# The threshold search over three engines, and a last attention step without its detour

## The chip, the cores and the metric

The kernel runs on one core of one Trainium2 chip. The time is that of one execution on the device, in microseconds (us). Three runs of the kernel before gave 870.73, 871.9 and 873.82 us, so the median is 871.9 us. TensorE is called PE below (its weight loads PEld), VectorE DVE, ScalarE ACT, GpSimd POOL, and SP issues the transfers.

## The reference, cut to what matters

Four layers, each an attention and a feed-forward part, are added to `x` (2 batches of 256 rows of 512 numbers). The change touches the third attention, and the search of the fourth attention that runs beside it.

```python
# third attention: 32 query heads of 128, 8 groups of keys and values, 512 context rows
q = rmsnorm((layernorm(x) @ q_proj_w.T).reshape(B, Q, 32, 128).transpose(0, 2, 1, 3))
k = rmsnorm(k of 8 groups, each repeated 4 times);  v = likewise, not normed
attn = softmax(q @ k.T * scale + mask)
x = x + concat_heads(attn @ v) @ o_proj_w.T
...
# fourth attention: for each of 512 columns, the 154 largest of the 512 context rows;
# those among the first 256 rows are the "crucial" channels
_, topk_idx = jax.lax.top_k(jnp.moveaxis(channel_map, 1, 2), 154)
```

The products of the third attention are done in three passes over a high and a low part of each operand (`PARTS`), both of type float32r.

## The kernel before, in words

**Steps.** `layer2_attention` (L1542) works in 16 steps, one for each of 8 head groups and 2 batches. Even and odd steps are the two batches of one group; the first (step 0) and the last (step 15) are written out, and steps 1 to 14 are a loop of seven bodies, each an odd and an even step (on DVE six bodies, then steps 13 and 14 written out). A step has 8 units: 4 heads by 2 tiles of 128 queries. For a unit, PE computes scores (`scores`, L1808), DVE adds the mask and takes the maximum (`maximum`, L2070, instruction L2075), ACT takes the exponentials and their sums (`exponentials`, L1960, L1966), PE turns the 128x512 probabilities with four transposes (`turn_probs`, L1821, L1826), ACT copies the turned ones out of PSUM as the high part (`probsT_high`, L1974) and DVE subtracts for the low part (`probsT_low`, L2087). After two units (one head, a pair) PE multiplies them with the values (`mix`, L1830), in the one bank `V`.

**Beside a step.** In the same units PE projects keys and values (`project_kv`), then queries (`project_q`) of the following step, and the heads of the step before onto `x` (`project_out`, L1784); `fill` (L1839) fixes the unit of each. PE turns the normed rows of keys and queries of the following step (`turn_rows`, L1799) through the one bank `R`. ACT copies and squares the projections (`copy_kv`, `copy_q`), POOL norms them (`norm`, L1678), ACT and DVE split the turned ones (`rowsT_high` L1956/L1958, `rowsT_low` L2065/L2068). ACT also takes high parts of the following weights (`kv_weights_high`, `q_weights_high` L1990, `o_weights_high`), and POOL subtracts for their low parts (L1665, L1669, L1675).

**Division.** The probabilities are divided after the mix. At unit 7 DVE inverts the eight sums (`invert`, L2081), SP stores the inverses in DRAM and loads them back spread over all partitions, ACT copies the mixed heads to SBUF (`copy_mixed`, L1980), and POOL multiplies and splits them into high and low (`scale_heads`, L1696, L1700, L1702), two heads at a time. `project_out` then runs in the following step. After step 15 this chain stands alone at the end, with 24 products of PE behind it and two additions to `x` (`add_out`, L2093).

**The search.** For each of 8 row tiles of the transposed context (128x512), DVE finds the value of the 154th largest by bisection on bits. A round is four `bisection_count`s (L2240) of two tiles, one instruction per tile (L2244: compare and sum), and a `bisection_update` (L2289) of five small instructions, of which L2294, L2296, L2298 and L2301 have two inputs in SBUF. There is one count per unit and an update in every fourth unit: two rounds a step, 28 in steps 0 to 13, one in step 14, and those ahead of the steps. Then `choose_piece` (L2260) marks the chosen ones, 5 pieces for each pair of tiles (L2267, L2271, L2275, L2278, L2282): the first pair in units 4 to 7 of step 14, the other three pairs in step 15.

**Order.** Each engine has its own queue in a fixed, handwritten order; a waiting instruction holds all behind it. On ACT, unit u runs: row copies and splits of the following step, `copy_mixed`, the exponentials of unit u+1, `probsT_high` of unit u, weight copies. On DVE: `probsT_low` of u-1, `rowsT_low`, the maximum of u+1, values, `add_out`, and the search last. On PE: the fill, `turn_probs` of u, scores of u+2 (from unit 6 on those of the following step, which need `rowsT_low` of the rows), `mix`, `turn_rows`. `LoopOwn` numbers the steps of the search on one semaphore.

## Time and profile before

| | us |
|---|---|
| median of 3 runs | 871.9 |
| span of the profiled execution | 875.2 |
| steps 1 to 14, one pair of steps | 65.8 to 67.3 |
| last step, from the last transposes of step 14 (741.7) to the last addition (792.9) | 51.2 |
| tail behind it, to the end | 82.3 |

The page of the profile gives PE 783.4 us busy (90% of the span), DVE 719.1 (82%), ACT 519.3 (59%) and POOL 428.5 (49%). In its 40 slices of 21.9 us, PE stands at 9 tenths or more from slice 13 to slice 34, then falls to 5 and 7 tenths, which is the last step:

```profile
PE   1976899858987999999999999999999999578878
DVE  7878998968788888888888888887887887955974
ACT  6864898747466756756656756756656656321421
POOL 3237087805226647646646746646646746531110
```

A busy digit tells only that an engine had work in a slice; which wait ends last must be read from the timeline of the instructions on either side of it.

### The profile page before, as it was taken

The numbers are of one execution on the slowest core, as the hardware profiler recorded it, in microseconds if no ns is written. First come the engines' busy times: TensorE is split into PE (matmuls) and PEld (weight loads), VectorE is DVE, ScalarE is ACT, GpSimd is POOL, SyncE is SP. The second block draws the span as 40 slices with busy tenths as digits, with TensorE's granted clock in tenths as the row PEclk, the third lists the DMA queues.
The fourth block names the chain that finished last, engine by engine and source line by source line (L and its number), as shares of the span: only waits on it lengthen the run. The fifth ranks groups of instructions, "written<-read, shape, count | busy, mean of one in ns | idle before, by whom it ended". The sixth has DMA issues, their size and how long they took to land. (4 is left out here: it accounts for less than half of the span.)

```text
span 875.2 us, 16429 instructions
## 1 busy us (share of the span) xinstructions
PE 783.4 (90%) x5146; PEld 634.7 (73%) x5146; DVE 719.1 (82%) x1732; ACT 519.3 (59%) x1408; POOL 428.5 (49%) x380
## 2 busy tenths in 40 slices
PE   1976899858987999999999999999999999578878
PEld 0474676534776898898898897898898898465446
DVE  7878998968788888888888888887887887955974
ACT  6864898747466756756656756756656656321421
POOL 3237087805226647646646746646646746531110
PEclk9999999979999999999999999999999999789899
DMA  8253246562203102102102202201200300103001
GB/s 304 93 193 121 75 150 207 163 187 80 96 2 97 50 26 95 50 24 96 48 24 80 64 24 74 70 24 52 92 24 28 116 24 25 48 25 117 1 0 49
DMA packets 39114, 68.23 MB, mean 78 GB/s; under 512 B 5729, under 2 KB 18593, under 8 KB 38946
## 3 DMA queue, kind: packets, MB, share of 16 engines
q1 hardware_dynamic: 39074, 67.73, 23.5%
q8 instruction: 21, 0.34, 0.2%
q14 instruction: 19, 0.16, 0.1%
HBM read 62.38 MB, written 5.34 MB: 77 GB/s over the span
## 5 line engine op out<-in xcount | busy, mean ns | idle before, releaser
L1966 ACT ACTIVATE layer_attention_probs<-xnT,stats 128x512 f32<-128x512 f32 x128 | 93.9, 734 | 137.8 <-DVE stats L2075 137.8
L2244 DVE TENSOR_SCALAR_CACHE_REDUCE xn<-ctxT,candidate 128x512 bf16<-128x512 f32 x240 | 168.8, 741 | 0.0
L1750 PE MATMUL bank<-layer_attention_keysT,layer_attention_queriesT 128*128 128x512 f32 x384 | 122.6, 428 | 5.0 <-DVE layer_attention_queriesT L2068 5.0
L2087 DVE TENSOR_TENSOR layer_attention_probsT<-bank,layer_attention_probsT 128x512 fp32r<-128x512 f32 x128 | 88.0, 688 | 39.8 <-ACT layer_attention_probsT L1974 38.3
L1750 PEld LDWEIGHTS bank<-layer_attention_probsT,layer_attention_values 128*128 128x128 f32 x768 | 99.7, 191 | 23.0 <-DVE layer_attention_probsT L2087 9.3
L1750 PE MATMUL bank<-layer_attention_probsT,layer_attention_values 128*128 128x256 f32 x768 | 103.4, 284 | 14.0 <-DVE layer_attention_probsT L2087 13.9
L1750 PE MATMUL bank<-layer_attention_wo,layer_attention_headsT 128*128 128x512 f32 x384 | 104.5, 417 | 3.0 <-issue 3.0
L1974 ACT CAST layer_attention_probsT<-bank 128x512 fp32r<-128x512 f32 x128 | 74.7, 584 | 50.4 <-PE bank L1826 50.1
L1696 POOL TENSOR_TENSOR layer_attention_mixed<-layer_attention_mixed,xnT 128x512 f32<-128x512 f32 x32 | 52.1, 1627 | 86.3 <-DMA xnT<-inverse_sums 82.8
L1750 PE MATMUL bank<-layer_attention_l_wq,layer_attention_xnT 128*128 128x512 f32 x384 | 93.5, 392 | 0.0
L1750 PE MATMUL bank<-layer_attention_l_wkv,layer_context_parts 128*128 128x256 f32 x720 | 90.5, 278 | 0.0
L1750 PEld LDWEIGHTS bank<-layer_attention_l_wkv,layer_context_parts 128*128 128x128 f32 x720 | 88.5, 188 | 2.7
L2075 DVE CUSTOM_DVE_ANT_0 xnT<-bank,layer_attention_mask 128x512 f32<-128x512 f32 x128 | 87.0, 680 | 0.6 <-PE bank L1750 0.5
L1750 PEld LDWEIGHTS bank<-layer_attention_wo,layer_attention_headsT 128*128 128x128 f32 x384 | 71.6, 196 | 17.5 <-issue 3.1
L1750 PEld LDWEIGHTS bank<-layer_attention_l_wq,layer_attention_xnT 128*128 128x128 f32 x384 | 70.9, 188 | 15.0 <-issue 0.2
L1826 PE MATMUL bank<-ident,layer_attention_probs 128*128 128x128 f32 x512 | 78.1, 276 | 3.6 <-ACT layer_attention_probs L1966 3.6
L1826 PEld LDWEIGHTS bank<-ident,layer_attention_probs 128*128 128x128 f32 x512 | 62.5, 142 | 15.2 <-issue 4.8
L1750 PEld LDWEIGHTS bank<-layer_attention_keysT,layer_attention_queriesT 128*128 128x128 f32 x384 | 63.7, 193 | 11.6 <-issue 5.8
L1681 POOL TENSOR_SCALAR layer_attention_ssq<-layer_attention_ssq 128x4 f32<-128x4 f32 x48 | 9.3, 193 | 90.6 <-ACT layer_attention_squares L1925 90.6
L1925 ACT ACTIVATE layer_attention_squares<-bank 128x128 f32<-128x128 f32 x192 | 51.9, 298 | 0.0
L1170 ACT ACTIVATE layer_attention_probs<-bank,layer_attention_negmax 128x512 f32<-128x512 f32 x64 | 44.9, 706 | 10.6 <-DVE layer_attention_negmax L1066 10.3
L1669 POOL TENSOR_TENSOR layer_attention_l_wq<-layer_attention_l_raw_qo,layer_attention_l_wq 128x2048 fp32r<-128x2048 f32 x8 | 36.9, 4616 | 28.3 <-ACT layer_attention_l_wq L1990 28.3
(322 smaller groups left out, 1673.0 us busy)
## 6 DMA issues: line engine op xcount, KB each, us to landing
layer_attention_l_raw_qo<-in_wqT SPq DMA_DIRECT2D x9, 1024.0 KB, 5.1
xnT<-inverse_sums SPq DMA_DIRECT2D x16, 512.0 KB, 3.7
layer_attention_l_raw_qo<-in_woT SPq DMA_DIRECT2D x8, 1024.0 KB, 7.1
tw_raw<-in_w_gateT SPq DMA_DIRECT2D x8, 688.0 KB, 5.2
tw_raw<-in_w_upT SPq DMA_DIRECT2D x8, 688.0 KB, 4.2
tw_raw<-in_w_downT SPq DMA_DIRECT2D x6, 768.0 KB, 4.7
layer_attention_l_raw_kv<-in_wkvT SPq DMA_DIRECT2D x9, 512.0 KB, 4.8
ternary<-tw_rounded SPq DMA_DIRECT2D x8, 344.0 KB, 2.6
```

Source lines behind the costliest of these rows:

```text
L1170: a.activation(probs[:, u % 4, :], S[u % 3][:, :], ACT.Exp, bias=negmax[:, tile(u), head(u):head(u) + 1], accum_out=sums[:, tile(u), head( ...
L1669: g.tensor_tensor(wq[:, 1], gw.raw_q[:, :, :], wq[:, 0], ALU.subtract).then_inc(gw.q_low, 1)
L1681: own(g.tensor_scalar(ssq[:, c, :], ssq[:, c, :], 1.0 / HD, EPS, ALU.mult, ALU.add))
L1696: g.tensor_tensor(now, now, factors, ALU.mult).then_inc(S_["mix_scaled"], 1)
L1750: last = pe.matmul(out, stationary[f][a], moving[f][b], start=f == 0 and x == 0, stop=f == count - 1 and x == 2)
L1826: last = pe.transpose(T[u % 2][:, c * P:(c + 1) * P], probs[:, u % 3, c * P:(c + 1) * P], k.ident[:, :])
L1925: return a.activation(squares[:, h, :], source, ACT.Square, accum_out=ssq[:, c, h:h + 1])
L1966: a.activation(probs[:, u % 3, :], masked[:, u % 2, :], ACT.Exp, bias=negmax[:, u:u + 1], scale=-1.0, accum_out=sums[:, u:u + 1]).then_inc ...
L1974: a.copy(probsT[:, 0, p % 2, :, u % 2 * P:(u % 2 + 1) * P], T[u % 2][:, :].rearrange("p (c q) -> p c q", c=CPB)).then_inc(S_["probsT_high" ...
L2075: v.tensor_tensor_reduce(masked[:, u % 2, :], S[u % 2][:, :], mask[:, u % TPB, :], -1.0, 3.4e38, ALU.add, ALU.min, negmax[:, u:u + 1]).the ...
L2087: v.tensor_tensor(probsT[:, 1, p % 2, :, columns], T[u % 2][:, :].rearrange("p (c q) -> p c q", c=CPB), probsT[:, 0, p % 2, :, columns], A ...
L2244: own(k.nc.vector.tensor_scalar((k.flags if flags is None else flags)[:, r % 2], row_tile(k.ctxT, r), k.candidate[:, r:r + 1].bitcast(F32) ...
```

## The change

- **Search in steps 1 to 10** (`SEARCHED` = 5 loop bodies of two steps). A body of 16 units has 5 rounds of 3 units, and unit 15 has none. DVE counts six tiles (`BY_DVE` = 3 counts). POOL compares the last two (`compare_aside`: two instructions, flags in bfloat16, in a new tile `aside`), and ACT sums the flags (`count_aside`: two activations with a sum). POOL's compare of round 0 is its first work of the odd step, that of round 1 stands behind `norm(following, 0)`, that of round 2 behind `norm(following, 1)`, that of round 3 behind `scale_heads` of the even step, that of round 4 behind its `norm(following, 0)`. ACT's sums stand behind `probsT_high` of units 0, 4 and 7 (odd step) and 2 and 5 (even step). DVE waits for them ahead of each update.
- **Steps 11 and 12**: one round each, a count in every second unit, the update in unit 7. **Steps 13 and 14**: the choice, two pairs of tiles a step, pieces at `u * 10 // 8`. Step 15 has neither. The number of rounds is the same (2 + 25 + 2 = 29).
- **Last step** (`run_final`). For each unit DVE inverts one column of sums and multiplies the identity by it (`divided`: a reciprocal, a wait for it, a 128x128 `diagonal`); PE turns the probabilities with a plain float32 product by that diagonal (`turn_divided`) in place of the transpose. The mix then comes out divided: ACT copies it from bank `V` as the high part (`head_high`), DVE subtracts (`head_low`), and PE projects head by head (`project_final`: 2 tiles by 3 products). SP's round trip, `copy_mixed` and `scale_heads` go for this step. `project_out` of step 14 stands in units 5 and 6.
- **Last output weights.** They come as a ninth group of the query weights (`wqT`), in place of a repeat of the first that was loaded and not used; the loads and splits of the last `woT` group go (SP, ACT L1996, POOL L1675).
- The loops of ACT and POOL are split in two, of 5 and 2 bodies; on DVE steps 11 to 14 are written out. `dynamic_dma_scratch_size` is set to 1024.

```diff
+    SEARCHED = 5
+    ROUNDS = 5
+    SLOTS = 3
+    BY_DVE = 3
-    CHOICE = {STEPS - 2: (0,), STEPS - 1: (2, 4, 6)}
+    CHOICE = {STEPS - 3: (0, 2), STEPS - 2: (4, 6)}
...
@@ gpsimd
+                def compare_aside(step, r):
+                    g.wait_ge(S_["bisection"], step[0] * OWN_BODY + (OWN_LOOP + r * ROUND_OPS))
+                    g.sem_inc(S_["stepped"], 1)
+                    for j in range(2):
+                        row = 2 * BY_DVE + j
+                        last = g.tensor_scalar(aside[:, j], row_tile(k.ctxT, row), k.candidate[:, row:row + 1].bitcast(F32), 1.0,
+                                               ALU.is_gt, ALU.mult)
+                    last.then_inc(S_["aside_flags"], 1)
...
+                    if searching and odd:
+                        compare_aside(step, 0)
                     if not first:
                         scale_heads(before, 0)
                         scale_heads(before, 1)
+                    if searching and not odd:
+                        compare_aside(step, 3)
                     if odd:
                         o_weights_low(step, 0)
-                    if not last:
-                        norm(following, own, KEYS)
+                    norm(following, own, KEYS)
                     if odd:
                         o_weights_low(step, 1)
-                    if last:
-                        return
                     norm(following, own, 0)
+                    if searching:
+                        compare_aside(step, 1 if odd else 4)
                     if not odd:
                         kv_weights_low(step)
                     norm(following, own, 1)
+                    if searching and odd:
+                        compare_aside(step, 2)
...
@@ tensor
+                def turn_divided(step, u):
+                    pe.wait_ge(S_["probsT_low"], at(step, UNITS, u - 1))
+                    pe.wait_ge(S_["diagonal_ready"], u + 1)
+                    for c in range(CPB):
+                        last = pe.matmul(T[u % 2][:, c * P:(c + 1) * P], probs[:, u % 3, c * P:(c + 1) * P],
+                                         diagonal[:, u % 2, :], start=True, stop=True)
+                    last.then_inc(S_["probsT_psum"], 1)
+
+                def project_final(step, h):
+                    pe.wait_ge(S_["final_low"], h + 1)
+                    for t in range(TPB):
+                        if h == 0:
+                            pe.wait_ge(S_["out_added"], added(after(step, -1), t + 1))
+                        for x, (a, b) in enumerate(PARTS):
+                            last = pe.matmul(J[t][:, :], finalT[:, a, h, t * P:(t + 1) * P], wq[:, b, h, :],
+                                             start=h == 0 and x == 0, stop=h == REP - 1 and x == 2)
...
+                def run_final(step):
+                    before = after(step, -1)
+                    for u in range(UNITS):
+                        turn_divided(step, u)
+                        if u + 2 < UNITS:
+                            scores(step, u + 2)
+                        if u == 0:
+                            mix(before, PAIRS - 1)
+                        if u in (3, 5, 7):
+                            mix(step, u // 2 - 1, final=True)
+                        if u in (5, 6):
+                            for half in range(2):
+                                project_out(before, u - 5, half, weights=wq)
+                    project_final(step, 0)
+                    mix(step, PAIRS - 1, final=True)
+                    for h in range(1, REP):
+                        project_final(step, h)
...
@@ scalar
+                def count_aside(step, r):
+                    a.wait_ge(S_["aside_flags"], step[0] * ROUNDS + (r + 1))
+                    for j in range(2):
+                        row = 2 * BY_DVE + j
+                        last = a.activation(aside[:, j], aside[:, j], ACT.Copy, accum_out=k.counts[:, row:row + 1])
+                    last.then_inc(S_["aside_counted"], 1)
...
+                def run_final(step):
+                    before = after(step, -1)
+                    for u in range(UNITS):
+                        if u == 1:
+                            copy_mixed(before, PAIRS - 1)
+                        if u + 1 < UNITS:
+                            exponentials(step, u + 1)
+                        probsT_high(step, u)
+                        if u in (3, 5, 7):
+                            head_high(step, u // 2 - 1)
+                    head_high(step, PAIRS - 1)
...
                         probsT_high(step, u)
+                        if searching and odd and u in (0, 4, 7):
+                            count_aside(step, (0, 4, 7).index(u))
+                        if searching and not odd and u in (2, 5):
+                            count_aside(step, 3 + (2, 5).index(u))
...
@@ vector
+                    r, part = divmod((step[1] - 1) * UNITS + u, SLOTS)
+                    if r < ROUNDS:
+                        bisection_count(k, own, part)
+                        if part == SLOTS - 1:
+                            v.wait_ge(S_["aside_counted"], step[0] * ROUNDS + (r + 1))
+                            bisection_update(k, own)
...
+                def divided(step, u):
+                    v.wait_ge(S_["exp_ready"], at(step, UNITS, u + 1))
+                    v.reciprocal(last_inverse[:, u:u + 1], sums[:, u:u + 1]).then_inc(S_["last_inverted"], 1)
+                    v.wait_ge(S_["last_inverted"], u + 1)
+                    v.tensor_scalar(diagonal[:, u % 2, :], k.ident[:, :], last_inverse[:, u:u + 1], None, ALU.mult)\
+                     .then_inc(S_["diagonal_ready"], 1)
...
+                def run_final(step):
+                    before = after(step, -1)
+                    for u in range(UNITS):
+                        if u:
+                            probsT_low(step, u - 1)
+                        else:
+                            probsT_low(before, UNITS - 1)
+                        divided(step, u)
+                        if u + 1 < UNITS:
+                            maximum(step, u + 1)
+                        if u in (4, 6):
+                            head_low(u // 2 - 2)
+                        if u == 7:
+                            add_out(before, 0)
+                    probsT_low(step, UNITS - 1)
+                    add_out(before, 1)
+                    head_low(2)
+                    head_low(3)
```

## Rows read from the trace of the kernel before

**Rows 1.** Windows: length, busy of PE, PEld, DVE, ACT, POOL, granted clock, DMA

```profile
639.00:706.00 67.00, 66.80 (x436) 59.50 (x435) 56.66 (x152) 41.97 (x127) 39.24 (x34) 1.00 0.17 55
742.00:792.00 50.00, 36.09 (x164) 29.71 (x162) 36.61 (x71) 13.95 (x29) 21.36 (x15) 0.80 0.12 40
```

**Rows 2.** Waits of PE from 306 to 742 us: total, times, longest

```profile
PE bank L1750 <- DVE layer_attention_probsT L2087: 5.0, 5, 1.6
```

**Rows 3.** Timeline (start, us, engine, line, [idle before]), end of step 10

```profile
605.92 4.62 POOL L1669 TENSOR_TENSOR layer_attention_l_wq<-layer_attention_l_raw_qo,layer_attention_l_wq 128x2048 fp32r<-128x2048 f32 x1 [3.54 <-ACT layer_attention_l_wq L1990]
...
609.81 0.75 DVE L2294 SCALAR_TENSOR_TENSOR enough<-counts,flip 128x8 f32<-128x8 f32 x1
...
611.08 1.49 DVE L2301 TENSOR_TENSOR candidate<-found,bits 128x8 int32<-128x8 int32 x1
...
613.82 1.67 PE L1750 MATMUL bank<-layer_attention_probsT,layer_attention_values 128*128 128x256 f32 x12 [1.49 <-DVE layer_attention_probsT L2087]
```

**Rows 4.** Timeline, step 4, units 4 to 6: ACT, DVE and PE

```profile
395.74 0.59 ACT L1974 CAST layer_attention_probsT<-bank 128x512 fp32r<-128x512 f32 x1 [1.06 <-PE bank L1826]
...
400.40 1.11 ACT L1990 CAST layer_attention_l_wq<-layer_attention_l_raw_qo 128x1024 fp32r<-128x1024 f32 x1
...
402.03 0.69 DVE L2068 TENSOR_TENSOR layer_attention_queriesT<-bank,layer_attention_queriesT 128x512 fp32r<-128x512 f32 x1 [0.74 <-ACT layer_attention_queriesT L1958]
...
402.87 0.93 PE L1750 MATMUL bank<-layer_attention_keysT,layer_attention_queriesT 128*128 128x512 f32 x3
```

**Rows 5.** Timeline, step 5, units 4 to 6: POOL, ACT and PE

```profile
430.24 1.04 POOL L1686 TENSOR_TENSOR xn<-xn,layer_attention_ssq 128x512 f32<-128x512 f32 x1
...
432.08 0.69 ACT L1956 ACTIVATE layer_attention_keysT<-bank,r_attention_norm_weights 128x512 fp32r<-128x512 f32 x1
...
435.78 0.59 ACT L1958 CAST layer_attention_queriesT<-bank 128x512 fp32r<-128x512 f32 x1 [0.32 <-PE bank L1805]
...
437.34 0.96 PE L1750 MATMUL bank<-layer_attention_keysT,layer_attention_queriesT 128*128 128x512 f32 x3
```

**Rows 6.** Timeline, ACT: two activations with a sum

```profile
183.30 0.63 ACT L1284 ACTIVATE layer_ffn_t<-xn 128x512 f32<-128x512 f32 x1 [2.86 <-PEq L919]
...
183.93 0.61 ACT L1284 ACTIVATE layer_ffn_t<-xn 128x512 f32<-128x512 f32 x1
```

**Rows 7.** Groups by line and form, POOL: count, busy us, mean ns

```profile
L398 POOL TENSOR_SCALAR tw_raw<-tw_raw,tw_winv 128x512 f32<-128x512 f32 x1 | 0.7, 688 | 0.1
...
L1686 POOL TENSOR_TENSOR xn<-xn,layer_attention_ssq 128x512 f32<-128x512 f32 x47 | 48.9, 1040 | 3.7
```

**Rows 8.** Timeline, PE: float32r products, then plain float32 ones

```profile
706.12 3.05 PE L1750 MATMUL bank<-layer_attention_wo,layer_attention_headsT 128*128 128x512 f32 x12
...
855.85 3.87 PE L2473 MATMUL bank<-tail_wra,xnT 128*128 128x136 f32 x32
```

**Rows 9.** Timeline, start of the last step: DVE, PE, ACT

```profile
741.56 2.83 DVE L2278 SCALAR_TENSOR_TENSOR ctxT<-ctxT,left 128x256 f32<-128x256 f32 x2
...
746.91 0.68 DVE L2087 TENSOR_TENSOR layer_attention_probsT<-bank,layer_attention_probsT 128x512 fp32r<-128x512 f32 x1
...
747.73 2.22 PE L1750 MATMUL bank<-layer_attention_probsT,layer_attention_values 128*128 128x256 f32 x12 [3.55 <-DVE layer_attention_probsT L2087]
...
748.22 0.72 ACT L1966 ACTIVATE layer_attention_probs<-xnT,stats 128x512 f32<-128x512 f32 x1 [5.27 <-DVE stats L2075]
...
749.54 0.69 DVE L2087 TENSOR_TENSOR layer_attention_probsT<-bank,layer_attention_probsT 128x512 fp32r<-128x512 f32 x1
...
750.88 0.72 ACT L1966 ACTIVATE layer_attention_probs<-xnT,stats 128x512 f32<-128x512 f32 x1 [0.52 <-DVE stats L2075]
```

**Rows 10.** Timeline, end of the last step: PE, DVE

```profile
779.12 1.64 PE L1750 MATMUL bank<-layer_attention_probsT,layer_attention_values 128*128 128x256 f32 x12 [1.49 <-DVE layer_attention_probsT L2087]
...
783.74 8.45 PE L1750 MATMUL bank<-layer_attention_wo,layer_attention_headsT 128*128 128x512 f32 x24 [2.98 <-issue]
...
792.23 0.69 DVE L2093 TENSOR_TENSOR x<-bank,x 128x512 f32<-128x512 f32 x1 [0.71 <-PE bank L1750]
```

More of the change, by code:

```diff
@@ L1828, in turn_probs, with mix @@
                     last.then_inc(S_["probsT_psum"], 1)
-                def mix(step, p):
-                    if not is_start(step) or p >= 1:
+                def mix(step, p, final=False):
+                    if final and p >= 1:
+                        pe.wait_ge(S_["final_low"], p)
+                    elif not is_start(step) or p >= 1:
                         pe.wait_ge(S_["mix_copied"], at(step, PAIRS, p))
@@ L1866, in run @@
-                def run(step, first=False, last=False):
+                            project_out(before, 1, 0, following)
+                            project_out(before, 1, 1, following)
+                def run(step, first=False):
                     following, before = after(step), after(step, -1)
                     for u in range(UNITS):
-                        fill(step, u, first, last)
+                        fill(step, u, first)
                         turn_probs(step, u)
@@ L1872, in run @@
                             scores(step, u + 2)
-                        elif not last:
+                        else:
                             scores(following, u + 2 - UNITS)
@@ L1915, in _ @@
                     run((i, 2))
-                run(final, last=True)
-                mix(final, PAIRS - 1)
-                for half in range(2):
-                    for t in range(TPB):
-                        project_out(final, t, half)
+                run_final(final)
             @block.scalar
@@ L2107, in run @@
                             invert(step)
-                        if not last and u in (6, 7):
+                        if u in (6, 7):
                             rowsT_low(following, TURNS[u - 5])
@@ L2170, in _ @@
                 run(start, first=True)
-                with v.Fori(0, STEPS // 2 - 2) as i:
+                with v.Fori(0, SEARCHED) as i:
                     run((i, 1))
                     run((i, 2))
-                run((None, STEPS - 3))
-                run((None, STEPS - 2))
-                run(final, last=True)
-                probsT_low(final, UNITS - 1)
+                for x in range(2 * SEARCHED + 1, STEPS - 1):
+                    run((None, x))
+                run_final(final)
                 for t in range(TPB):
```

191 lines of the change are left out of this document (109 added, 82 removed).

## The prediction

> **What bounds the kernel now.** I read the windows first. Over steps 12 and 13 PE is busy 66.8 of 67 us at the full granted clock, while DVE has 56.7, ACT 42.0 and POOL 39.2 [rows 1]. So PE bounds the steps of the loop: work that leaves DVE there is worth nothing by itself, and what counts is whether PE has to wait. The list of waits says how often it does: five times in 436 us, 5.0 us in all, each time for `probsT_low` of DVE [rows 2]. The timeline shows where: at the end of an even step, ahead of the last `mix`. POOL is in a 4.62 us subtraction; DVE's L2294, 8 numbers long, ends just as POOL does (0.75 us), and L2301 is held 1.49 us by POOL's next instruction; PE then idles 1.49 us [rows 3]. The last step is another case. PE is busy 36.1 of 50 us there, at a mean clock of 0.80, DVE 36.6 [rows 1]; DVE carries three of the four choices and the chain of divisions by DRAM and POOL stands at its end: the low part of the last unit is ready at 779.1, the last addition ends at 792.9 [rows 10].
>
> **The loop, what goes.** Unit 15 has no count and no update now, so DVE reaches the last `probsT_low` of an even step some 3 us earlier (two counts and an update, of which 0.75 and 1.49 us alone are waiting [rows 3]). The five waits of rows 2 lie behind steps 4, 8 and 10 (1.55, 1.53, 1.49 us) and 2 and 12 (0.2 each). All but that of step 12 go: **-4.8 us**. What is late next there is nothing: PE is then bound by itself.
>
> **The loop, what is added on ACT.** A sum costs the pitch of two such activations, 183.93 - 183.30 = 0.63, so two tiles cost 1.24 us [rows 6]. Most of the five places have idle time of ACT behind them. Two do not, because the turned rows of queries of the following step come out there, and PE needs them in unit 6 (scores of the following step).
>
> *Even step, unit 5.* From 395.74, when PE releases it, to the split of the queries' rows at 401.35 ACT has no gap; the new sum stands in that run, between the copy that begins at 399.93 and the weight copy at 400.40. Behind it `rowsT_low` runs from 402.03 to 402.72, and PE starts the scores that need it at 402.87 [rows 4]. There is no slack: ACT's run starts from PE, and all of it shifts. The sum adds 1.24 us to PE in each of five steps: **+6.2 us**. POOL's flags are long ready by then (its `norm` ends at 396.6). Bounds: 0, if half the sum could hide in a gap I don't see, to 1.6 us each.
>
> *Odd step, unit 4.* Here ACT also waits. POOL ends `norm(following, 0)` at 430.24 + 1.04 = 431.28 [rows 5] and then compares two tiles. The nearest row is a one-input operation of 512 columns, 0.69 us; as upper bound I take the two-input one, 1.04 [rows 7]. With 0.69 the flags are there at 432.7, the sum ends at 433.95. ACT was at the split of the keys' rows at 432.08, and from there ran without a gap to 435.46 (0.32 idle ahead of 435.78), 3.38 us [rows 5]. So it gets to the queries' rows at 437.3, DVE's low part follows 0.62 later and takes 0.69 (as in rows 4: 401.35 to 402.03 to 402.72), and is done at 438.6. PE wanted it at 437.34 [rows 5]: 1.3 us, five times: **+6.5 us**. With 1.04 a compare it is 2.0, and if POOL's instruction also holds DVE's update, 2.6; the lower bound is 0, if ACT's run has gaps that give it back.
>
> Queued behind ACT's waiting sum are the rows' splits, the exponentials of unit 6 and the high part of unit 5; DVE's splits and PE wait for those. POOL is no bound: it gets 5 x 2 x 0.69 = 7 us more on 39 of 67. The other three sums shift `copy_mixed` and an exponential by about a microsecond that PE doesn't wait for. DVE's updates, at new units, can be held by POOL as in rows 3, but no `mix` waits behind them; I put them at 0 (to +1 us a body).
>
> A rule speaks against the compare on POOL. The Trainium skill, GPSIMD Engine Reference, section 7 (Performance pitfalls), has bodies that produce a truth value at 2.03 cycles per element against 1.03 when unrolled. By an estimate from that page 512 elements at 1.2 GHz would be 0.87 us; the odd step would then cost 1.7 instead of 1.3 us, 2 us more in all. No row here has a compare on POOL; the nearest one above has 0.69.
>
> **Steps 11 to 14.** Fewer counts in 11 and 12: nothing, PE bounds. In 13 and 14 the pieces take about the place of the counts, but those with two inputs are held by POOL: 2.83 us for two [rows 9]. In unit 3 of step 13 two such pieces meet POOL's weight subtraction; DVE has about that much slack to PE's next turn. **+0.3 us** (0 to 3).
>
> **The last step.** It starts alike, since two pieces and two additions stand ahead of it on DVE as before: the last low part of step 14 begins at 746.91 [rows 9].
> - The first turn now waits for its diagonal. A column's reciprocal, the wait for it and 128 columns: 0.45 us (estimate; 0.3 to 0.8, the upper end if POOL holds the scaling). The turn is a plain float32 product: 16 of 136 columns take 3.87 us [rows 8], so four of 128 take 0.91, against 0.36. The last `mix` of step 14 is queued behind the first turn and scores, and at half clock starts at about 750.6, not 747.73 [rows 9]. ACT's copy of it stands ahead of the exponentials of unit 2, which begin at 753.4, not 750.88. That is a new wait of 2.5 us.
> - Then one unit follows the other by this cycle: exponentials to low part 1.32 (748.22 to 749.54), low part 0.60, diagonal 0.45, maximum to exponentials 0.71: 3.08 us. Exponentials of unit 5 at 762.6, low part of unit 4 at 763.9, turn of unit 5 at 765.1.
> - From there PE bounds: a product of 512 columns takes 0.243 ((3.05 - 0.16)/12, rows 8; the 0.16 is the drain). Turn 0.91, scores 0.78, mix 1.41, six plus six products 2.93, turn 0.91, again 2.93, turn 0.91: 10.9, to 776.0.
> - High and low part of unit 7 and the addition of step 14 take 2.1; then half of head 0 (0.73), mix 1.41, three heads 4.4, the last addition 0.9: to 785.5. Before, it was 792.9: -7.4 us.
> - The clock: 0.80 over 50 us is some 20 us at 1.2 instead of 2.4 GHz [rows 1]. The new step keeps PE busier from 765 on, but between 748 and 765 it is still busy for only three quarters. Two stretches at half clock, one of which holds `head_high` and so an exponential: +1.7. POOL's `scale_heads` of step 14 over one or two diagonals: +0.7.
>
> Together **-5.0 us** (-8 to +1). SP's loads, the copy and the subtractions of the last `woT` group lay beside other work: 0. The tail is untouched.
>
> **The sum.** -4.8 + 6.2 + 6.5 + 0.3 - 5.0 = +3.2 us. On the span of the profiled execution, 875.2, that is 878.4; the median of the runs stood 3.3 us below that execution, so **875 us**.
>
> **The rivals.**
> - *The sums cost PE nothing* (the rows' splits wait for PE's transposes anyway, and the run of ACT has gaps). For it: the split in step 5 had 0.32 us of idle ahead, and ACT is busy 42 of 67 us. Against: rows 4. Then the loop gains 4.8 and the last step 5 to 7: 861 to 862 us. That is the other side; it decides if less than about 1 us of the 2.5 per body reaches PE.
> - *Half of them reach PE*: ACT's run starts earlier since DVE's update left unit 3 of the odd step, or the sum of bfloat16 is shorter. 6 us less: 869.
> - *The last step gains nothing*: half clock throughout makes PE the bound at 4.8 us a unit. 880 us.
> - *POOL holds DVE.* Each update has four instructions with two SBUF inputs, and in the loop they stand now where POOL works, the last one of round 4 some 0.3 us ahead of the 4.62 us subtraction. If it is caught, five times 3 us: 890 us. The rows bear it: L2301 was caught three times in six. The Trainium skill, GPSIMD Engine Reference, section 8 (Key points), says the same of the shared interfaces and DVE instructions with two SBUF inputs; rows 3 agree (0.75 and 1.49 us for 8 numbers).
>
> **How the numbers follow.** Chances: forecast 0.42 (its own range 872 to 880), sums free 0.24, half of them 0.17, last step without gain 0.08, POOL holding DVE 0.09. 0.3% (2.6 us) is about what a measurement can tell here. Faster, under 869.3: 0.24 and a third of the half case, 0.30. Within: the rest of that and a quarter of the forecast, 0.22. Slower: 0.48. Range 861 to 883: it leaves out the held updates and a part of the first rival.
>
> **What would show it.** PE waits for `rowsT_low` (L2068 before) ahead of the scores in unit 6 of each searched step, near 1.2 us in even and 1.3 in odd ones; none ahead of the `mix` at an even step's end; a body of two steps near 68.4 us instead of 65.8 to 67.3; ACT idle in odd unit 4 until POOL's compare. In the last step: turns of 0.9 us, units 3 us apart, from the last low part to the last addition some 8 us instead of 14. It is wrong if bodies take 65.8 us, or if POOL's compare takes over 1.1 us.

## The result, and the profile after

The changed kernel takes **911.1 us** (median of 4 runs, 908.8 to 913.3) against 872.9 us of the kernel before beside it: ratio 1.044, 95% interval 1.041 to 1.047. Forecast were 875 us, and 883 as the upper end. The direction was the likeliest of the three, the size is outside the range.

The page of the changed kernel (span 907.0 us). First busy time, share and instructions by engine, then two groups (busy us, mean ns, idle before):

```profile
PE 793.7 (88%) x5172; PEld 642.9 (71%) x5178; DVE 685.7 (76%) x1651; ACT 547.9 (60%) x1507; POOL 517.4 (57%) x422
...
L1723 POOL TENSOR_SCALAR layer_attention_aside<-ctxT,candidate 128x512 bf16<-128x512 f32 x50 | 99.6, 2002 | 2.8 <-DVE candidate L2441 0.9
...
L2068 ACT ACTIVATE layer_attention_aside<-layer_attention_aside 128x512 bf16<-128x512 bf16 x50 | 31.1, 624 | 42.3 <-POOL layer_attention_aside L1723 42.3
```

POOL's compare takes **2.00 us**, where [rows 7] had been read as 0.69, and ACT's sums stood behind it for 42.3 us in all. The sum itself, 0.62, is that of [rows 6].

Where the time went, by the start of the step's reciprocal on DVE (the last one is `invert` of step 14): steps 1 to 10 took 331.5 us and take 375.3 (+43.8); steps 11 to 14 133.2 and 131.2 (-2.0); from there to the last addition 54.2 and 46.1 (-8.1); the rest -2. The bodies of the loop take 74.3 to 75.8 us, 75.1 in the mean; before they took 65.4 to 67.3 (the first one, 65.4, is below the range given ahead). An even step and the odd one behind it:

```profile
387.99 0.19 DVE L2175 RECIPROCAL stats<-stats 128x8 f32<-128x8 f32 x1
...
423.87 0.19 DVE L2175 RECIPROCAL stats<-stats 128x8 f32<-128x8 f32 x1
...
462.26 0.19 DVE L2175 RECIPROCAL stats<-stats 128x8 f32<-128x8 f32 x1
```

That is 35.9 us for an even and 38.4 for an odd step. The waits of PE between 290 and 830 us (total, times, longest), against [rows 2]:

```profile
PE bank L1837 <- DVE layer_attention_keysT L2159: 17.3, 5, 3.5
PE bank L1877 <- DVE layer_attention_diagonal L2247: 9.0, 4, 5.1
PE bank L1779 <- DVE layer_attention_queriesT L2162: 8.3, 5, 1.7
PE bank L1779 <- DVE layer_attention_values L2152: 6.1, 6, 1.8
...
PE bank L1779 <- DVE layer_attention_probsT L2181: 0.2, 1, 0.2
```

The waits for `probsT_low` at the ends of even steps are gone but for 0.2 us behind step 12, as forecast. The largest new one is five times 3.5 us. The timeline of POOL, ACT and PE in units 4 and 5 of step 5 shows the chain, against [rows 5]:

```profile
449.56 3.99 POOL L1723 TENSOR_SCALAR layer_attention_aside<-ctxT,candidate 128x512 bf16<-128x512 f32 x2
...
453.58 0.63 ACT L2068 ACTIVATE layer_attention_aside<-layer_attention_aside 128x512 bf16<-128x512 bf16 x1 [5.11 <-POOL layer_attention_aside L1723]
...
454.82 0.67 ACT L2021 ACTIVATE layer_attention_keysT<-bank,r_attention_norm_weights 128x512 fp32r<-128x512 f32 x1
...
456.41 1.11 PE L1837 MATMUL bank<-ident,xn 128*128 128x128 f32 x4 [3.45 <-DVE layer_attention_keysT L2159]
457.17 2.91 PE L1779 MATMUL bank<-layer_attention_wo,layer_attention_headsT 128*128 128x512 f32 x6
...
487.65 1.65 PE L1779 MATMUL bank<-layer_attention_wo,layer_attention_headsT 128*128 128x512 f32 x6
```

POOL ends its two compares at 453.55; ACT idles 5.11 us, sums, and only then splits the keys' rows; DVE's low part follows, and PE, which needs the bank `R` for the next rows, stands 3.45 us. The row at 457.17 is a second price. Six products take 2.91 us here and 1.65 in the even step. PE is at 1.2 GHz when it goes on, in step 5 from 456.41 to 461.89: it takes 5.5 us for what takes 3.0 at full clock, 2.5 us lost. It is so in steps 5, 7 and 9 (mean granted clock 0.90 over 35 us); in steps 1 and 3 half clock lasts half as long (0.95). Windows of the changed kernel (columns as in [rows 1]), two around such waits (steps 3 and 5) and one without:

```profile
372.00:407.00 35.00, 31.52 (x198) 27.81 (x198) 26.16 (x68) 19.52 (x65) 24.17 (x19) 0.95 0.13 45
441.00:476.00 35.00, 30.54 (x179) 26.47 (x178) 25.31 (x72) 18.01 (x57) 25.25 (x21) 0.90 0.13 45
407.00:441.00 34.00, 32.33 (x210) 28.60 (x209) 24.98 (x68) 25.72 (x76) 30.05 (x22) 1.00 0.20 62
```

The waits for `values` have another cause. DVE's update of round 0 now stands ahead of `values_low`, and POOL's subtraction of the output weights holds it:

```profile
439.68 2.41 POOL L1687 TENSOR_TENSOR layer_attention_wo<-layer_attention_l_raw_qo,layer_attention_wo 128x1024 fp32r<-128x1024 f32 x1
...
440.52 1.60 DVE L2434 SCALAR_TENSOR_TENSOR enough<-counts,flip 128x8 f32<-128x8 f32 x1
...
444.40 3.02 PE L1779 MATMUL bank<-layer_attention_l_wq,layer_attention_xnT 128*128 128x512 f32 x12 [1.02 <-DVE layer_attention_values L2152]
```

`enough`, 0.17 us long where nothing holds it, takes 1.4 to 2.4 us in each odd step, until POOL's subtraction ends, and PE stands 6.1 us in all behind it. The kernel before had the same hold (2.3 us in each odd step), but no `values_low` stood behind it.

A sum of steps 1 to 10: PE waits 33.9 us now and 5.5 before (+28.4), and is busy 341.2 us against 325.8 (+15.4); together that is the 43.8. It is busy for 22.9 us at half clock, which loses half of that, 11.4. The other 4.0 us of busy time I did not place.

The last step, against [rows 9, 10]: the first division, one cycle, and the end.

```profile
783.15 2.83 DVE L2418 SCALAR_TENSOR_TENSOR ctxT<-ctxT,left 128x256 f32<-128x256 f32 x2
786.01 1.96 DVE L2422 TENSOR_TENSOR ctxT<-xn,ctxT 128x256 f32<-128x256 bf16 x2
...
789.71 2.04 PE L1877 MATMUL bank<-layer_attention_diagonal,layer_attention_probs 128*128 128x128 f32 x8 [5.08 <-DVE layer_attention_diagonal L2247]
...
799.30 0.69 DVE L2181 TENSOR_TENSOR layer_attention_probsT<-bank,layer_attention_probsT 128x512 fp32r<-128x512 f32 x1 [1.35 <-ACT layer_attention_probsT L2039]
...
802.34 0.69 DVE L2181 TENSOR_TENSOR layer_attention_probsT<-bank,layer_attention_probsT 128x512 fp32r<-128x512 f32 x1 [1.35 <-ACT layer_attention_probsT L2039]
...
817.89 0.69 DVE L2181 TENSOR_TENSOR layer_attention_probsT<-bank,layer_attention_probsT 128x512 fp32r<-128x512 f32 x1 [2.00 <-ACT layer_attention_probsT L2039]
...
825.10 1.37 DVE L2187 TENSOR_TENSOR x<-bank,x 128x512 f32<-128x512 f32 x2 [2.61 <-PE bank L1888]
```

The cycle is 3.04 us (forecast 3.08), the last low part to the end of the last addition 8.6 us (forecast 8, before 14).

### The profile page after: what moved, and what is told of

It reads as the page before. It is cut to its first block and busy times, and to the rows that moved or that the text cites. A ratio compares the mean times of both kernels' runs of the same rounds, so it can differ in the third digit from the quotient of the medians.

```text
span 907.0 us, 16587 instructions
## 1 busy us (share of the span) xinstructions
PE 793.7 (88%) x5172; PEld 642.9 (71%) x5178; DVE 685.7 (76%) x1651; ACT 547.9 (60%) x1507; POOL 517.4 (57%) x422
## 5 line engine op out<-in xcount | busy, mean ns | idle before, releaser
L2384 DVE TENSOR_SCALAR_CACHE_REDUCE xn<-ctxT,candidate 128x512 bf16<-128x512 f32 x190 | 133.7, 741 | 0.0
L1779 PE MATMUL bank<-layer_attention_probsT,layer_attention_values 128*128 128x256 f32 x768 | 100.7, 280 | 1.4 <-DVE layer_attention_probsT L2181 1.4
L1723 POOL TENSOR_SCALAR layer_attention_aside<-ctxT,candidate 128x512 bf16<-128x512 f32 x50 | 99.6, 2002 | 2.8 <-DVE candidate L2441 0.9
L2039 ACT CAST layer_attention_probsT<-bank 128x512 fp32r<-128x512 f32 x128 | 74.7, 583 | 35.8 <-PE bank L1858 29.1
L1779 PE MATMUL bank<-layer_attention_wo,layer_attention_headsT 128*128 128x512 f32 x336 | 94.5, 426 | 0.0
L1708 POOL TENSOR_TENSOR layer_attention_mixed<-layer_attention_mixed,xnT 128x512 f32<-128x512 f32 x30 | 49.2, 1641 | 45.7 <-DMA xnT<-inverse_sums 38.4
L1858 PE MATMUL bank<-ident,layer_attention_probs 128*128 128x128 f32 x480 | 74.1, 278 | 0.4 <-ACT layer_attention_probs L2031 0.4
L1779 PEld LDWEIGHTS bank<-layer_attention_wo,layer_attention_headsT 128*128 128x128 f32 x336 | 63.6, 200 | 12.5
L1858 PEld LDWEIGHTS bank<-ident,layer_attention_probs 128*128 128x128 f32 x480 | 59.5, 143 | 11.2 <-issue 1.6
L270 POOL TENSOR_TENSOR rstd<-varep,minus_half 128x1 f32<-128x1 f32 x24 | 15.1, 639 | 90.9 <-DVE varep L226 63.0
L2068 ACT ACTIVATE layer_attention_aside<-layer_attention_aside 128x512 bf16<-128x512 bf16 x50 | 31.1, 624 | 42.3 <-POOL layer_attention_aside L1723 42.3
```

Of the source, the lines that this page charges most:

```text
L270: g.tensor_tensor(k.rstd[:, t:t + 1], k.varep[:, t:t + 1], k.minus_half[:, 0:1], ALU.pow).then_inc(k.tile_rstd, 1)
L1708: g.tensor_tensor(now, now, factors, ALU.mult).then_inc(S_["mix_scaled"], 1)
L1723: last = g.tensor_scalar(aside[:, j], row_tile(k.ctxT, row), k.candidate[:, row:row + 1].bitcast(F32), 1.0, ALU.is_gt, ALU.mult)
L1779: last = pe.matmul(out, stationary[f][a], moving[f][b], start=f == 0 and x == 0, stop=f == count - 1 and x == 2)
L1858: last = pe.transpose(T[u % 2][:, c * P:(c + 1) * P], probs[:, u % 3, c * P:(c + 1) * P], k.ident[:, :])
L2039: a.copy(probsT[:, 0, p % 2, :, u % 2 * P:(u % 2 + 1) * P], T[u % 2][:, :].rearrange("p (c q) -> p c q", c=CPB)).then_inc(S_["probsT_high" ...
```

## The experiments

Theory 1: the loss is the compare's 2.00 us, with ACT standing behind it in order. Rival 2: the sums on ACT. Rival 3: POOL's extra work holds DVE, or POOL's own norms come late. All twelve kernels, each against the kernel before on the same chip:

| kernel | median us | ratio, 95% interval |
|---|---|---|
| e1, other compare forms | 903.6 (one run) | |
| e2, no compares | 868.9 | 0.995 (0.993 to 0.997) |
| e3, compares, no sums | 892.1 | 1.020 (1.017 to 1.024) |
| e4, DVE counts all | 870.9 | 0.997 (0.995 to 1.000) |
| e5, compare at 0.70 us | 879.9 | 1.008 (1.006 to 1.010) |
| e6, other forms again | 891.0 (one run) | |
| e7, sign and sum on ACT | 878.0 | 1.004 (1.001 to 1.007) |
| e8, e4 with earlier pieces | 868.0 | 0.994 (0.991 to 0.996) |
| e9, search of before, new last step | 866.3 | 0.992 (0.988 to 0.995) |
| e10, e3 with a later update | 877.0 | 1.003 (1.001 to 1.005) |
| e11, e8 without the division | 866.6 | 0.993 (0.989 to 0.996) |
| e12, e8 with a mixed search | 865.0 | 0.991 (0.988 to 0.994) |

**e1 and e6: what makes the compare slow.** `compare_aside` takes another form in each of the five rounds:

```diff
-  last = g.tensor_scalar(aside[:, j], row_tile(...), candidate, 1.0, ALU.is_gt, ALU.mult)
+  # e1: is_gt | is_gt, mult to f32 | subtract | subtract to f32 | is_gt 0.5, mult to f32
+  # e6: mult | min, max | add, mult | subtract, mult | mult 0.5, add 1.0
```

> The five compares of a body on POOL take five other forms, the threshold left as it is or not used: round 0 is_gt alone to bfloat16, round 1 is_gt and mult to float32, round 2 a subtraction to bfloat16, round 3 a subtraction to float32, round 4 is_gt of a fixed number and mult to float32 (so the counts of rows 6 and 7 are not those of the reference's search). The changed kernel has is_gt and mult to bfloat16 at 2.00 us each. If the truth value is what costs, the subtractions take 0.7 us and the three others near 2.0. If the output in bfloat16 costs, rounds 0 and 2 take 2.0 and rounds 1, 3 and 4 take 0.7. If the second operation costs, rounds 0, 2 and 3 are the cheap ones. If it is the threshold read per partition, only round 4 is cheap. If POOL needs 2.0 us for any such operation when it meets DVE's work, all five take 1.5 to 2.5 with a wide spread. Bodies of two steps get shorter than 75.1 us by as much as rounds 1 and 2 get cheaper.

> Five more forms in the place of the compares, all to bfloat16 (counts of rows 6 and 7 are not true ones): round 0 a product by the threshold alone, round 1 min and max, round 2 addition and product, round 3 subtraction and product, round 4 product and addition of two fixed numbers. In the kernel before, L396 (min, max) took 0.76, L398 (product, addition) 0.69 and L400 (addition, product) 0.62 us for 512 columns; is_gt alone and a subtraction alone took 1.58 and 1.57 here. If the operation decides: rounds 0, 1, 2 and 4 take 0.6 to 0.8 and round 3 takes 1.6 to 2.0. If a single operation is the slow form: round 0 takes 1.6 and round 3 takes 0.7. If it is the place: all take 1.5 to 2.0.

Groups of POOL between 290 and 700 us, e1 and then e6:

```profile
L1728 POOL TENSOR_SCALAR layer_attention_wide<-ctxT,candidate 128x512 f32<-128x512 f32 x10 | 19.9, 2000 | 0.5
L1734 POOL TENSOR_SCALAR layer_attention_wide<-ctxT 128x512 f32<-128x512 f32 x10 | 19.1, 1929 | 0.4
L1730 POOL TENSOR_SCALAR layer_attention_aside<-ctxT,candidate 128x512 bf16<-128x512 f32 x10 | 15.6, 1572 | 0.0
L1732 POOL TENSOR_SCALAR layer_attention_wide<-ctxT,candidate 128x512 f32<-128x512 f32 x10 | 15.6, 1565 | 0.0
...
L1726 POOL TENSOR_SCALAR layer_attention_aside<-ctxT,candidate 128x512 bf16<-128x512 f32 x8 | 12.5, 1582 | 0.0
```

```profile
L1731 POOL TENSOR_SCALAR layer_attention_aside<-ctxT,candidate 128x512 bf16<-128x512 f32 x10 | 19.9, 2003 | 0.0
L1725 POOL TENSOR_SCALAR layer_attention_aside<-ctxT,candidate 128x512 bf16<-128x512 f32 x8 | 12.5, 1573 | 0.0
L1727 POOL TENSOR_SCALAR layer_attention_aside<-ctxT,candidate 128x512 bf16<-128x512 f32 x10 | 6.8, 687 | 0.5
L1729 POOL TENSOR_SCALAR layer_attention_aside<-ctxT,candidate 128x512 bf16<-128x512 f32 x10 | 6.8, 692 | 0.5
L1733 POOL TENSOR_SCALAR layer_attention_aside<-ctxT 128x512 bf16<-128x512 f32 x10 | 6.0, 622 | 0.4
```

The output's type does nothing (2.00 and 2.00; 1.57 and 1.57), the threshold by partition 0.07 us. Nor is it the truth value: a subtraction or a product alone costs the same 1.57 as `is_gt` alone. Three levels are seen: 0.62 to 0.69 us for the pairs min/max, add/mult and mult/add; 1.57 for any of the three single operations; 1.93 to 2.00 for a pair with `is_gt` or `subtract` in it. Neither of the simple hypotheses (operation, or single form) holds alone. Each form keeps within 0.05 us of itself at its place, and e5 has the fast form at all five places, so meeting DVE is not the cause. L398, which the forecast was priced by, is a mult/add pair: the fastest level. The forecast also weighed the Trainium skill, GPSIMD Engine Reference, section 7 (Performance pitfalls), by which a truth value would be the dear body (0.87 us as an estimate): here the measured 1.57 us of the product alone and 2.00 us of subtraction and product say otherwise.

The two kernels also tell the rounds apart. e1 keeps 2.00 us in round 1, the one in odd unit 4, and PE still stands five times 3.45 us for `keysT`. In e6 that round takes 0.69 and the wait falls to 0.3 to 0.8 us, but with rounds 0 and 3 at 1.57 and 2.00 bodies still take 71.2 us, and PE stands up to 2.0 us for `queriesT` in even steps.

**e2 and e3: compare or sum.**

```diff
 e2:                                        e3:
-  last = g.tensor_scalar(aside[:, j], ...) -  a.wait_ge(S_["aside_flags"], ...)
-  last.then_inc(S_["aside_flags"], 1)      -  last = a.activation(aside[:, j], ..., accum_out=...)
+  g.sem_inc(S_["aside_flags"], 1)          -  v.wait_ge(S_["aside_counted"], ...)
```

> POOL's compares are left out (the flags are zeros, written once), POOL only passes the signal on; ACT's sums, DVE's wait for them and everything else stay. Theory 1 (the loss is ACT standing behind a compare of 2.0 us that it has to wait for, and the half clock that follows): ACT's wait in odd unit 4 goes, bodies fall from 75.1 to about 68.4 us as the forecast's sums alone would have it, 873 to 880 us. Rival 2 (the sums on ACT are themselves the loss): bodies stay above 73, over 900 us. Rival 3 (POOL's extra work holds DVE's instructions with two inputs): also faster, to 865 to 880, but then the next kernel, which keeps the compares, stays slow.

> POOL's compares stay, at the same places and with the same wait for DVE's update (they read a constant threshold); ACT's sums and DVE's wait for them are left out, so rows 6 and 7 are not counted. Theory 1: nobody waits for POOL's flags, bodies fall to 65.8 to 67 us, 860 to 868 us. Rival 2 gives the same. Rival 3 (POOL's 4 us more per round delay its own norms and hold DVE): bodies stay above 72 us, over 895 us.

e2 has 868.9 us: rival 2 falls. It is faster than theory 1 said, too: bodies take 67.0 us and not 68.4, since of the sums only those in the even steps reach PE, five times 1.0 to 1.1 us. But e3, in which nobody waits for POOL's flags, has 892.1 and bodies of 71.0: by theory 1 it should have had 860 to 868, and it comes near to what rival 3 said. Its even steps take 38.6 us. The timeline of POOL, DVE and PE at the end of step 6 says why:

```profile
487.02 4.57 POOL L1681 TENSOR_TENSOR layer_attention_l_wq<-layer_attention_l_raw_qo,layer_attention_l_wq 128x2048 fp32r<-128x2048 f32 x1
487.15 4.48 DVE L2433 TENSOR_TENSOR found<-found,set_bit 128x8 int32<-128x8 int32 x1
...
493.32 0.94 PE L1779 MATMUL bank<-layer_attention_keysT,layer_attention_queriesT 128*128 128x512 f32 x3 [2.48 <-DVE layer_attention_queriesT L2158]
```

An instruction of DVE on 8 numbers, 0.17 us long elsewhere, stands for as long as POOL's subtraction. That is the forecast's rival "POOL holds DVE", at the place that it named, in a kernel of which it did not speak. At this place the changed kernel escapes by luck: its last update in step 6 ends at 498.46, 0.1 us ahead of the start of POOL's subtraction (498.57). At another place it is caught, in the odd steps, as shown above.

**e10: the held update by itself.** e3 with the update of the fifth round moved:

```diff
-  if part == SLOTS - 1:
+  if part == SLOTS - 1 and r < ROUNDS - 1:
       bisection_update(k, own)
+  if step[1] == 2 and u == UNITS - 1:
+      bisection_update(k, own)
```

> The kernel with POOL's compares and without ACT's sums (892.1 us), with DVE's update of the fifth round moved from unit 6 to the end of the even step. In that kernel an update instruction of 8 numbers took 4.48 us, as long as POOL's subtraction of the query weights (4.57 us) that had started 0.13 us ahead of it. If POOL holding DVE there is what costs that kernel its time: the 4.5 us instruction goes, even steps fall from 38.6 to about 34 to 35 us, and the time to 868 to 876 us. If POOL's later norms cost it: no change, 888 to 893.

892.1 becomes 877.0, even steps fall from 38.6 to 32.8. So 15 of the 19 us by which e3 was slower than the kernel before came from one instruction meeting another; 877.0 is 1 us above the expected range. The rest is in the odd steps (35.0 us, 32.4 in e3), where PE waits 5 times, 7.9 us in all, for `values_low`. The moved update is held 1.59 us by the end of the subtraction of the query weights, and the next one stands through that of the output weights:

```profile
426.66 2.40 POOL L1687 TENSOR_TENSOR layer_attention_wo<-layer_attention_l_raw_qo,layer_attention_wo 128x1024 fp32r<-128x1024 f32 x1
426.70 2.38 DVE L2431 SCALAR_TENSOR_TENSOR enough<-counts,flip 128x8 f32<-128x8 f32 x1
```

The Trainium skill, GPSIMD Engine Reference, section 8 (Key points), says that POOL shares its SBUF interfaces with DVE and contends with DVE's instructions that have two SBUF inputs; the 4.48 us beside POOL's 4.57 agree with it.

**e5: the forecast at its own price.**

```diff
-  last = g.tensor_scalar(aside[:, j], row_tile(...), candidate, 1.0, ALU.is_gt, ALU.mult)
+  last = g.tensor_scalar(aside[:, j], row_tile(...), candidate, 0.0, ALU.mult, ALU.add)
```

> POOL's compares become a product by the threshold and an addition of 0 (the instruction form of L398, the row that the forecast took its 0.69 us from), at the same places; ACT sums them as before, so rows 6 and 7 have no true counts. If the forecast failed by the price alone, each takes 0.7 us instead of 2.00, a body takes 66.5 to 68.4 us instead of 75.1 and the kernel 868 to 878 us. If it is POOL's order (a wait for DVE's update in front of its norms), whatever the compare costs, bodies stay above 71 us and the kernel above 885. If this form too takes 1.6 to 2.0 us here, POOL pays for the place (ctxT, DVE and ACT at work), not for the operation: then over 900.

POOL's group over the whole trace, then the timeline of step 5, an odd one of 33.6 us: POOL's two products and PE's two waits:

```profile
L1723 POOL TENSOR_SCALAR layer_attention_aside<-ctxT,candidate 128x512 bf16<-128x512 f32 x50 | 34.3, 698 | 0.9 <-DVE candidate L2441 0.9
```

```profile
437.86 1.37 POOL L1723 TENSOR_SCALAR layer_attention_aside<-ctxT,candidate 128x512 bf16<-128x512 f32 x2
...
442.09 0.65 PE L1837 MATMUL bank<-ident,xn 128*128 128x128 f32 x4 [0.30 <-DVE layer_attention_keysT L2159]
...
445.52 0.94 PE L1779 MATMUL bank<-layer_attention_keysT,layer_attention_queriesT 128*128 128x512 f32 x3 [0.94 <-DVE layer_attention_queriesT L2162]
```

The span is 880.5 us; the forecast said 878.4. PE waits 0.30 + 0.94 = 1.24 us in this odd step (forecast 1.3), for `queriesT` 1.0 to 1.3 in even ones (1.24), bodies take 68.4 to 69.8 us, 68.8 in the mean (68.4), and the granted clock stays 1.00 through the loop from 279 us on. In the odd steps from 3 on `enough` takes 0.2 us at most, and the waits for `values` are gone. The median of 879.9 is 2 us above the expected range. So the price of the compare alone, 1.3 us fifty times, makes 31 us between the medians (911.1 and 879.9), 26.5 between the spans.

**e7: no POOL, ACT compares by itself.**

```diff
-  last = a.activation(aside[:, j], aside[:, j], ACT.Copy, accum_out=k.counts[:, row:row + 1])
+  last = a.activation(aside[:, j], row_tile(k.ctxT, row), ACT.Sign, scale=-1.0,
+                      bias=k.candidate[:, row:row + 1].bitcast(F32), accum_out=signed[:, j:j + 1])
+  own(v.tensor_scalar(k.counts[:, 6:8], signed[:, :], -0.5, 256.0, ALU.mult, ALU.add))
```

> POOL does nothing for the search. ACT forms the sign of (threshold - value) for its two tiles and sums it in the same instruction, and DVE turns the two sums into counts with one more small instruction per round. Theory 1 (the loss is POOL's price): ACT's 2 x 0.62 us a round stay, POOL's waits go: as the kernel without compares, bodies 66.5 to 67.5 us, 866 to 873 us. If changing between the sign and the exponentials makes ACT load something each time, its two sums take several us more per round: over 890 us.

878.0 us, between the two cases. Nothing is loaded between the functions: the trace has one ACT_TABLE_LOAD, at 0.8 us of the span, and the sign takes 0.73 us against 0.62 for the copy. But even steps take 35.7 to 35.8 us, and PE waits five times, 9.2 us in all, for `queriesT`: ACT's place in the even step is the narrow one.

**e4, e8, e9, e12: the last step without the loop's loss.** In e4 DVE counts 3, 3 and 2 tiles; e8 ends each step's pieces by unit 6; e9 takes the search of before; e12 mixes the two:

```diff
 e4
+  for row in range(3 * part, min(3 * part + 3, 8)):
+      own(v.tensor_scalar(flags, row_tile(k.ctxT, row), candidate, 0.0, ALU.is_gt, ALU.add, accum_out=...))
 e8
-  pieces[u * len(pieces) // UNITS:(u + 1) * len(pieces) // UNITS]
+  pieces[min(u * len(pieces) // 7, len(pieces)):min((u + 1) * len(pieces) // 7, len(pieces))]
 e12: rounds of three units in bodies 1, 2 and steps 11, 12; of four units in bodies 3 to 5
```

> Nothing on POOL and ACT: DVE counts all eight tiles of a round in three units (3, 3 and 2), rounds and places otherwise as in the changed kernel, and its last step. DVE gets 2 x 5 x 0.74 = 7.4 us more per body on about 52 of 67. Theory 1 and rival 2: bodies of 66 to 68 us if DVE stays behind PE, with the last step's 8 us kept: 860 to 872 us. If DVE is then late for PE's turns: bodies over 70 us, 880 to 890 us.

> The kernel in which DVE counts everything in three units, with the pieces of the row choice in steps 13 and 14 all done by unit 6 of a step instead of unit 7, so that two pieces (4.17 us, held by POOL's scale_heads) no longer stand ahead of the first division. If PE's wait of 5.2 us for the first diagonal comes from them: it falls to 1 to 2 us, and the time to 866 to 869 us from 870.9. If the pieces are then held in unit 6 and delay step 14's own low parts: no change, 870 to 872.

> Steps 0 to 12 search as the kernel before does, DVE alone, a round in four units, so that three of the thirty rounds are left out (the limit is coarser by three bits); the pieces of the row choice in steps 13 and 14 and the last step are those of the changed kernel. If the last step's gain read from the traces (8.1 us) stands by itself and the loop is as before: 863 to 867 us. If the sum is as the forecast had the last step (5.0 us): 867 to 870. If the move of the pieces costs it: 872 or more.

> The 868.0 us kernel with its 30 rounds laid out otherwise, all by DVE: three units a round only in the first two bodies and in steps 11 and 12, four units a round (as in the kernel before) in the other three bodies. Bodies with four rounds took 65.8 to 66.1 us, those with five 66.6 to 67.8. If that difference is DVE's, three bodies give back 1 us each, less up to 1 us in steps 11 and 12: 865 to 866.5 us. If it is only where POOL's and DVE's work happen to meet, 866 to 870.

e4 shows that POOL's and ACT's help was not needed: DVE does all counts in bodies of 66.9 us (66.3 before). e9, which searches three rounds fewer, prices the last step and the pieces alone: 7 us under the kernel before, with the loop at 330.6 us against 331.5 and the last step 46.7 against 54.2. e8's first division waits 1.19 us instead of 5.2, and the granted clock is 1.00 over the last step:

```profile
750.12 1.13 PE L1869 MATMUL bank<-layer_attention_diagonal,layer_attention_probs 128*128 128x128 f32 x8 [1.19 <-DVE layer_attention_diagonal L2239]
```

```profile
744.00:787.00 43.00, 35.80 (x218) 30.17 (x217) 22.32 (x55) 14.62 (x34) 11.43 (x7) 1.00 0.04 13
```

From `invert` of step 14 to the last addition e8 takes 41.9 us and e4 47.5; steps 1 to 10 happened to take 2 us longer in e8's profiled execution (336.3 against 334.3), with the same code there, and steps 11 to 14 took 133.0 against 131.0. The medians are 2.9 us apart and their intervals overlap. e12 has the lowest median, 865.0 us; its interval overlaps that of e8, so the mixed search is not shown to be the better one. Both are under the kernel before, by 0.6 and 0.9%.

**e11: what the division costs.** e8 with transposes by `ident` instead of the products with the diagonal; it leaves out the division of the last step:

```diff
-  last = pe.matmul(T[u % 2][...], probs[:, u % 3, ...], diagonal[:, u % 2, :], start=True, stop=True)
+  last = pe.transpose(T[u % 2][...], probs[:, u % 3, ...], k.ident[:, :])
```

> The 868.0 us kernel with plain transposes (by ident) in the last step instead of products with the diagonal; DVE still makes the diagonals and PE still waits for them, so that only the turn's own price goes and the last step's probabilities are not divided. Turns 0.36 instead of 0.88 us. If the unit's cycle holds the turn (3.05 us a unit): 8 x 0.5 = 4 us faster, 864 us. If the turn lies beside ACT and DVE: within 1 us, 867 to 869.

866.6 against 868.0, and from `invert` of step 14 to the last addition 41.8 against 41.9 us. The four products of a unit take 0.88 us where the transposes take 0.36, and PE has waits for the diagonal around them: from one diagonal to the next it is 3.05 us in both traces. So the division is free while the chain by ACT and DVE bounds, which excludes the 4 us. It is not free where PE bounds: from the seventh diagonal to the eighth e8 takes 5.75 us and e11 4.80. In the totals this doesn't show, since e11's profiled execution ran part of the last step at half clock (mean 0.93 from 742 to 790 us), where one such distance took 4.32 us.

## Why the prediction was wrong

- **The step that failed: "odd step, unit 4", by the price of POOL's compare.** 0.69 us, at most 1.04, from rows of other operations; it takes 2.00. The two bounds did not enclose the value: both were rows of 512 columns, neither had an `is_gt`. The text named "over 1.1 us" as what would prove it wrong, but gave that no place in the range. By its own working, 2 x 1.3 us later in unit 4 would have added 2.6 us a body, 888 us, so that even the corrected price leaves part out:
- **The clock after the wait was left out.** In each body PE stands 3.45 us and then falls to 1.2 GHz, which loses 11.4 us in the loop. It also fell after waits of 2.5 us (e3, four of five), 2.0 us (e6, three of five) and 1.9 us (e7, two of five), and not behind those of 0.3 to 1.3 us of e5.
- **The held updates were put at 0, because no `mix` waits behind them.** `values_low` does, in the odd steps, and PE stands 6.1 us for it. So "POOL holds DVE" (0.09, 890 us) does happen in the changed kernel, at a place that the forecast did not name; e3 and e10 show it at the place given, at 15 us in all.
- **The place of the wait was one turn too late.** The forecast followed ACT to the queries' rows and the scores of unit 6. But ACT's sum also stands ahead of the split of the keys' rows, and PE waits for their low part before it can turn the next rows. In the kernel before there was 1 us between the two:

```profile
433.43 0.75 DVE L2065 SCALAR_TENSOR_TENSOR layer_attention_keysT<-bank,r_attention_norm_weights,layer_attention_keysT 128x512 fp32r<-128x512 f32 x1
...
435.15 0.60 PE L1805 MATMUL bank<-ident,xn 128*128 128x128 f32 x4
```

- **Right: the direction and the mechanism, ACT in order behind POOL's compare.** With the forecast's price e5 comes near its numbers, span 880.5 against 878.4, but in part by luck. Its steps 1 to 10 cost 12.4 us more than before where the forecast had 7.9, and its last step gains 7.1 where the forecast had 5.0. Rival "sums free" holds for half: without a compare ahead (e2) the sums of odd steps cost nothing, those of even steps 1.0 to 1.1 us.
- **Right: what goes at the ends of even steps.** Only that of step 12 is left, with 0.2 us.
- **Slips without weight:** (3.05 - 0.16)/12 is 0.241, and the stretch where PE bounds adds up to 10.8 us, not 10.9.
- **The last step gained 8.1 us, not 5.0.** Cycle, turn (0.9) and end were as worked out. The two deductions did not come: only some 3 us around the first `mix` ran at half clock, and POOL met one diagonal (0.51 us instead of 0.29). Ahead of the first division PE waits 5.1 us, for two pieces (four instructions, 4.8 us) that POOL holds; e8 brings that wait down to 1.2.
- **The search shared by three engines** was aimed at DVE, which did not bound: e4 does without it in 66.9 us a body. It took POOL from 39 to 59 us of work in a body.

## What to carry to other kernels

Price an added instruction by a row with the same operations, not only the same shape; where there is none, the range must reach to a multiple. Follow a wait it causes to everything in the queue behind it, and to what the clock does then. Before work is moved to another engine, ask whether the first one bounds: here DVE had room, and ACT had to wait in order behind POOL. A small DVE instruction with two SBUF inputs belongs ahead of or behind POOL's long ones, never just after their start, and least of all ahead of a part that PE needs.

## What was not expected of the hardware

POOL's TENSOR_SCALAR on 512 columns has three prices: 0.62 to 0.69 us for min/max, add/mult, mult/add, 1.57 for `mult`, `subtract` or `is_gt` alone, 1.93 to 2.00 for `is_gt` or `subtract` followed by `mult`. Adding a second operation to the product makes it faster, 0.69 against 1.57. ACT's sign with a sum (0.73 us) stands among exponentials without a table load between them. PE was at half clock after single waits of 3.5 us, and after some of 1.9 to 2.5 us, in loops that otherwise ran at full clock. A DVE instruction on 8 numbers took 4.48 us beside a subtraction of POOL of 4.57 us that had started 0.13 us earlier.
